# Inverse roots by one power on GpSimd in place of Newton steps on VectorE, in a fused cross-attention and FFN kernel

## The reference

```python
def _layernorm(x, axis=-1, eps=1e-05):
    m, v = mean(x), var(x)
    return (x - m) / sqrt(v + eps)

def simple_rmsnorm(x):
    n = maximum(norm(x, axis=-1), 1e-12)
    return x / n * sqrt(d)

def bitlinear158(x, w):          # rows to 8 bits by their largest value, weights to -1, 0, 1
    xn = simple_rmsnorm(x)
    return activation_quant(xn) @ weight_quant(w).T

x = x + cross_attention(layernorm(x), ctx)        # 16 heads, softmax over 64 keys
x = x + bitlinear158(gelu(bitlinear158(layernorm(x), w1)), w2)
```

## Time and profile before

| | us |
|---|---|
| median of 3 executions | 471.61 |
| the three executions | 467.57, 472.11, 471.61 |
| span of the profiled execution | 470.1 |
| PE busy in it | 399.1 (85%) |
| DVE busy | 344.6 (73%) |
| ACT busy | 257.7 (55%) |
| POOL busy | 218.9 (47%) |

### The profile page before, as it was taken

The page is one execution under the profiler, slowest core; times in us unless marked ns, Lnnn a source line. Parts: engine busy times, 40 slices in busy tenths (PEclk is TensorE's granted clock), DMA queues, the critical chain, the costliest instruction groups (busy, mean ns, idle before and its releaser), DMA issues.

```text
span 470.1 us, 8743 instructions
## 1 busy us (share of the span) xinstructions
PE 399.1 (85%) x2775; PEld 277.9 (59%) x2775; DVE 344.6 (73%) x909; ACT 257.7 (55%) x472; POOL 218.9 (47%) x269
## 2 busy tenths in 40 slices
PE   0998887989789897999999999999999997776463
PEld 0465754667557573767676767676767674464221
DVE  1805654788978896978787878787878788977663
ACT  0223244534276854676858585858485858555430
POOL 1000001445455474465655646474747474857551
PEclk9999998999899998999999999999999999999765
DMA  8950436431212323243425252434345343444435
GB/s 272 350 159 20 205 120 199 135 92 48 57 47 59 82 69 82 62 106 74 108 65 114 59 115 64 107 82 93 81 92 83 91 97 77 104 125 79 100 67 91
DMA packets 65085, 48.55 MB, mean 103 GB/s; under 512 B 51216, under 2 KB 56592, under 8 KB 64016
## 3 DMA queue, kind: packets, MB, share of 16 engines
q1 hardware_dynamic: 62656, 41.70, 36.4%
q10 hardware_dynamic: 2384, 6.29, 4.0%
HBM read 31.72 MB, written 4.46 MB: 77 GB/s over the span
## 4 chain that ended last, share of the span: by engine, by line
issue 41%; POOL 36%; PE 5%; DMA 3%; DVE 2%; POOLq 1%; SPq 1%; ACT 0%; DVEq 0%
POOL cl L529 10%; POOL tq L550 7%; POOL qb L553 6%; POOL yc L537 3%; POOL xa L542 3%; POOL xn L293 3%; POOL xq L545 3%; DMA qt<-qb 1%; DMA rinv_d<-ri 1%; DMA rb<-rinv_d 1%; POOLq L184 1%; PE hps L778 1%; PE ps L692 1%; PE ps L694 1%; PE hps L708 1%
## 5 line engine op out<-in xcount | busy, mean ns | idle before, releaser
L529 POOL TENSOR_TENSOR cl<-cr,ch 128x512 fp32r<-128x512 f32 x64 | 83.4, 1325 | 166.3 <-ACT ch L602 166.3
L692 PE MATMUL ps<-xh,ah 128*128 128x256 f32 x256 | 75.6, 295 | 7.1 <-ACT g L617 4.5
L746 PE MATMUL hps<-bh,ch 128*128 128x256 f32 x256 | 75.8, 296 | 1.3 <-POOL cl L529 1.3
L586 ACT ACTIVATE qf<-ps 128x512 f32<-128x512 f32 x64 | 37.5, 586 | 68.0 <-PE ps L694 68.0
L694 PE MATMUL ps<-xh,al 128*128 128x256 f32 x256 | 72.4, 283 | 0.0
L693 PE MATMUL ps<-xl,ah 128*128 128x256 f32 x256 | 72.3, 282 | 0.0
L748 PE MATMUL hps<-bh,cl 128*128 128x256 f32 x256 | 71.5, 279 | 0.0
L747 PE MATMUL hps<-bl,ch 128*128 128x256 f32 x256 | 71.4, 279 | 0.0
L602 ACT ACTIVATE ch<-cr 128x512 fp32r<-128x512 f32 x64 | 39.3, 631 | 56.8 <-DVE cr L866 56.8
L692 PEld LDWEIGHTS ps<-xh,ah 128*128 128x128 f32 x256 | 49.2, 192 | 29.2 <-issue 28.7
L778 PE MATMUL hps<-w2q,qt 128*128 128x256 bf16 x256 | 37.4, 295 | 19.8 <-DMA qt<-qb 15.1
(11 more groups left out here) (129 smaller groups left out, 812.3 us busy)
## 6 DMA issues: line engine op xcount, KB each, us to landing
rb<-rinv_d SPq DMA_DIRECT2D x64, 256.0 KB, 4.0
out<-yo SPq DMA_DIRECT2D x32, 128.0 KB, 3.8
wq_s<-wq ACTq DMA_DIRECT2D x2, 1024.0 KB, 12.1
wo_s<-wo_t SPq DMA_DIRECT2D x1, 2048.0 KB, 9.0
w_s<-w_t SPq DMA_DIRECT2D x2, 1024.0 KB, 5.3
xs<-x SPq DMA_DIRECT2D x2, 1024.0 KB, 5.0
xs<-x ACTq DMA_DIRECT2D x1, 1536.0 KB, 14.6
wk_a<-wk_t ACTq DMA_DIRECT2D x2, 512.0 KB, 9.2
```

The source lines that it names most:

```text
L529: pool.tensor_tensor(cl[:, u % 2, :, b * S:(b + 1) * S], cr[:, :, b * S:(b + 1) * S], ch[:, u % 2, :, b * S:(b + 1) * S].bitcast(F32), ALU ...
L692: pe.matmul(o, ah[:, c, cols], xh[:, k % 2, c, :], start=(c == 0), stop=False)
L746: pe.matmul(O[:, 0:D], c_h, bh[:, hp, :], start=(hp == 0), stop=False)
```

## The change

Both functions move from VectorE to POOL, and the shift and Newton steps become one `tensor_tensor` with the power operation, whose second operand is a tile of -0.5 (`mhalf`). The floor that was a tile (`least`) becomes a constant per half, so that the floor and the last multiplication are one instruction for each half. `norms` is now ahead of `x_round` in the same even steps; `reciprocal_deviations(1)` follows `norm_x` of tiles 2 and 3, and `(2)` is in step 12, between `norms(3)` and `x_round`. A step's norms are 4 or 6 instructions, x's deviations 4.

```diff
-        def reciprocal_deviations(dve, part):
+        def reciprocal_deviations(pool, part):
...
-            dve.tensor_scalar(nw[0][:, c], mv[:, c, 1], EPS_LN, None, ALU.add).then_inc(sem["rstd_steps"], 1)
-            dve.wait_ge(sem["rstd_steps"], n)
-            rsqrt(dve, nw[0][:, c], rstd[:, c], nw[1][:, c], sem["rstd_steps"], n)
-            dve.scalar_tensor_tensor(out=nmean[:, c], in0=mv[:, c, 0], scalar=-1.0, in1=rstd[:, c], op0=ALU.mult, op1=ALU.mult).then_inc(sem["rstd_steps"], 1)
+            pool.tensor_scalar(nw[0][:, c], mv[:, c, 1], EPS_LN, 1.0, ALU.add, ALU.mult).then_inc(sem["rstd_steps"], 1)
+            pool.tensor_scalar(nw[1][:, c], mv[:, c, 0], -1.0, 0.0, ALU.mult, ALU.add).then_inc(sem["rstd_steps"], 1)
+            pool.wait_ge(sem["rstd_steps"], n + 1)
+            pool.tensor_tensor(rstd[:, c], nw[0][:, c], mhalf[:, 0:c.stop - c.start], ALU.pow).then_inc(sem["rstd_steps"], 1)
+            pool.wait_ge(sem["rstd_steps"], n + 3)
+            pool.tensor_tensor(nmean[:, c], nw[1][:, c], rstd[:, c], ALU.mult).then_inc(sem["rstd_steps"], 1)
...
+                def norms(j):
...
+                    for h, floor in halves:
+                        pool.tensor_scalar(v[:, 2 * h:2 * h + 2], stat[:, j, 2 * h:2 * h + 2], floor, 1.0, ALU.max, ALU.mult).then_inc(done, 1)
+                    n += len(halves)
+                    pool.wait_ge(done, n)
+                    pool.tensor_tensor(r[:, c], v[:, c], mhalf[:, c], ALU.pow).then_inc(done, 1)
+                    pool.wait_ge(done, n + 1)
+                    pool.tensor_tensor(t[:, c], r[:, c], amax[:, j, c], ALU.mult).then_inc(done, 1)
+                    pool.wait_ge(done, n + 2)
+                    for h, floor in halves:
+                        pool.tensor_scalar(scl[:, j, 2 * h:2 * h + 2], t[:, 2 * h:2 * h + 2], EPS_Q, wfactor[:, h:h + 1], ALU.max, ALU.mult).then_inc(done, 1)
...
+                reciprocal_deviations(pool, 1)
                 for n in range(LAST):
+                    if n % 2 == 0 and 0 <= (n - 6) // 2 < NB + 2:
+                        norms((n - 6) // 2)
+                    if n == 12:
+                        reciprocal_deviations(pool, 2)
                     if n % 2 == 0 and tile(n - 6):
                         x_round(n - 6)
                         x_round(n - 5)
...
-                    if n % 2 == 0 and 0 <= (n - 6) // 2 < NB + 2:
-                        norms((n - 6) // 2)
-                    if n == 11:
-                        reciprocal_deviations(dve, 2)
                     if tile(n):
                         row_max(n)
```

More of the change, by code:

```diff
@@ L48 @@
 QC = 16
[L49 to L51 removed]
+RSTD_STEPS = 4
 KR = 8
@@ L55, with norm_count @@
 LAST = NT + 10
-NORM_STEPS = RSQRT_OPS + 3
+def norm_count(j):
+    return sum(6 if 2 <= i < NB else 4 for i in range(j + 1))
 def build(nc, x, kv, wq, wk_t, wqr, wkr_t, wkv, wo_t, w1_t, w2_t, consts, out):
@@ L91, in build @@
         stat, amax, scl = [sb(n, [P, NB + 2, 4], F32) for n in ("stat", "amax", "scl")]
-        least, wfactor = [sb(n, [P, 4], F32) for n in ("least", "wfactor")]
+        wfactor = sb("wfactor", [P, 2], F32)
+        mhalf = sb("mhalf", [P, 16], F32)
         level = sb("level", [P, 4], F32)
@@ L184, in at_least @@
                 e.wait_ge(s, value)
[L186 to L199, removed]
         XPARTS = [0, 4, 16, NT]
@@ L327, in _ @@
                 pool.memset(ones[:, :], 1.0).then_inc(sem["const_set"], 1)
-                for k, w in ((0, D), (1, F)):
-                    pool.memset(least[:, 2 * k:2 * k + 2], EPS_N ** 2 * (EPS_LN * D ** 2 if k == 0 else 1.0) / w).then_inc(sem["eps_set"], 1)
+                pool.memset(mhalf[:, :], -0.5).then_inc(sem["eps_set"], 1)
                 pool.memset(level[:, 0:2], -1.0 / 127.0).then_inc(sem["eps_set"], 1)
@@ L553, in g_round @@
                     pool.tensor_scalar(qb[:, t % 2, :], tq[:, :], 1.0, -MAGIC, ALU.mult, ALU.add).then_inc(sem["g_rounded"], 1)
+                def norms(j):
+                    c = slice(2 if j >= NB else 0, 2 if j < 2 else 4)
+                    halves = [(h, thr) for h, thr in ((0, LEAST1), (1, LEAST2)) if c.start <= 2 * h < c.stop]
+                    v, r, t = fw[0], fw[1], fw[2]
+                    done, n = sem["norm_steps"], norm_count(j) - 2 * len(halves) - 2
+                    if j == 0:
+                        pool.wait_ge(sem["w_mean_steps"], 2)
+                    if j < NB:
+                        pool.wait_ge(sem["x_squared"], 2 * j + 2)
+                        pool.wait_ge(sem["x_maxima"], 2 * j + 2)
+                    if j >= 2:
+                        pool.wait_ge(sem["g_squared"], 2 * j - 2)
+                        pool.wait_ge(sem["g_maxima"], 2 * j - 2)
+                    at_least(pool, done, n)
+                    for h, floor in halves:
[8 more added lines that the diff above has]
+                        pool.tensor_scalar(scl[:, j, 2 * h:2 * h + 2], t[:, 2 * h:2 * h + 2], EPS_Q, wfactor[:, h:h + 1], ALU.max, ALU.mult).then_inc(done, 1)
                 def ternary(k):
@@ L895, in g_scale @@
                     dve.reciprocal(c2[:, c], gm[:, c]).then_inc(sem["g_scale_steps"], 1)
[L897 to L901, removed]
[L902 to L914 removed]
                 def finish(t):
                     dve.wait_ge(sem["products"], t + 1)
[L918 removed]
+                    dve.wait_ge(sem["norm_steps"], norm_count(t // 2 + 2))
                     at_least(dve, sem[f"out_stored{t % 2}"], 16 * (t // 2))
@@ L927, in w_means @@
                     dve.tensor_scalar(wmean[:, 0:2], total, 1.0 / (F * D), EPS_Q, ALU.mult, ALU.max).then_inc(sem["w_mean_steps"], 1)
[L928 to L930 removed]
+                    dve.tensor_scalar(wfactor[:, 0:2], total, 1.0 / (F * D * 127.0), EPS_Q / 127.0, ALU.mult, ALU.max).then_inc(sem["w_mean_steps"], 1)
                     dve.wait_ge(sem["w_mean_steps"], 1)
                     dve.reciprocal(wscale[:, :], wmean[:, 0:2]).then_inc(sem["w_mean_steps"], 1)
[L933 removed]
+                    dve.wait_ge(sem["w_mean_steps"], 3)
                 def ternary(n):
```

38 lines of the change are left out of this document (11 added, 27 removed).

## The result

| | kernel before | changed kernel |
|---|---|---|
| median of 7 runs | 471.6 us (467.57 to 472.11) | 474.08 us (472.85 to 475.21) |
| profiled execution | span 470.1, clock 0.958 | 474.39, span 472.3, clock 0.958 |

The ratio is 1.0064 (95% interval 1.0037 to 1.009): the changed kernel is slower, by 3.0 us according to the ratio (2.5 between the medians), where 5.2 us less were forecast. VectorE's busy time fell from 344.6 to 293.9 us, as predicted; GpSimd's (POOL) rose from 218.9 to 263.3.

A forecast was written before the change was run, and what follows sets the result against it. PE was taken to bound the steady steps, with VectorE's inverse root just hidden there. The terms 0.6 - 0.7 - 0.4 + 4.3 - 0.8 + 0.7 + 1.5 gave 5.2 us gained, 471.6 to 466.4 us; range 462 to 480.

The forecast's parts named there:

- Part 1: Before the loop: part 0 of x's deviations is hidden by the weight stage on either engine, worth nothing.
- Part 2: Step 0: without the twelve-column inverse root VectorE takes the scores earlier, a gain of 0.6 us.
- Part 3: Step 11: 2.8 us of waiting at L768 and 1.5 us of low clock behind it vanish, together 4.3.
- Part 4: POOL, even steps: 2.0 us norms delay row maxima through SP's queue; steps 6, 8, 12 lose 0.7, 0.4, 0.8; 30 gains 0.7.
- The rooms: SP's queue: slack before POOL's delay reaches the row maxima; 0.9 us in step 6, 1.2 in 8, 3.7 in 14 to 28.
- rival A: POOL, head of even steps: slow power, passed on by SP's queue, makes it slower; 482 us at 4 us norms; chance 0.2.
- Part 5: Last steps: VectorE's maxima of g no longer wait behind an inverse root, a gain of 1.5 us.
- signs of being wrong: Power on POOL above about 1.5 us, new PE gaps before L728 in even steps, or step 11's wait persisting with another releaser.
- B: Step 12: the wait and clock loss of step 11 move here, so no change, 469.9 us; chance 0.25.

The follow-up runs named there:

- e4: Changed kernel with every power in norms and deviations replaced by a multiplication, so it computes other numbers: 464.37 us, ratio 0.9844.
- e2: Changed kernel with only the third part of the deviations (step 12) moved behind x_round, norms still ahead: 468.78 us, ratio 0.9969.
- e5: Changed kernel with SP's queue issuing the row maxima ahead of x's transposes in even steps 0 to 12, POOL untouched: 465.42 us, ratio 0.9897.
- e11: Changed kernel with the norms' power run once more into a spare tile in steps 14 to 28: 479.95 us, ratio 1.0194.
- e6: Changed kernel with norms and deviations behind x_round, and row maxima ahead of x's transposes in even steps 0 to 12: 461.11 us, ratio 0.9776.
- e8: Kernel before, with only SP's queue order changed: row maxima ahead of x's transposes in even steps 0 to 12: 472.67 us, ratio 1.0028.
- e12: Kernel before, with norms and deviations kept as Newton steps on VectorE but moved behind the residual: 547.53 us, ratio 1.1615.
- e7: Kernel before, with only the deviations moved to POOL (step 12 behind x_round), norms staying Newton steps on VectorE: 467.84 us, ratio 0.9917.
- e1: Changed kernel with norms and the third part of the deviations moved behind the two x_round calls of an even step: 461.15 us, ratio 0.9804.

## Why the prediction was wrong

The measured 474.1 us lies inside the stated range of 462 to 480, on the other side of the kernel before than the forecast: the range was wide enough, the sum had the wrong sign.

**Parts 1 to 3** hold. Part 1: the first power (four columns) took 1.02 us like the others and nothing shifted with it. The Trainium skill (GPSIMD Engine Reference, section 2.1, Instruction dispatch) has some 6 us for the first call to a freshly loaded kernel; no row shows it. Part 2: from the start of the scores of step 0 to the shift it takes 6.41 to 6.42 us in the four kernels with the twelve-column steps on VectorE and 5.84 to 5.89 us in the ten with them on POOL, 0.56 gained where 0.6 was predicted; only the whole time up to there varies too much to show it. Part 3: 2.8 us at L768 and 1.55 us of clock behind it measured, 2.8 and 1.5 predicted, with the same granted clock of 1.00 up to the next wait.

**Part 4 is the step that failed.** Its mechanism was the right one, a queue that hands POOL's delay to the row maxima, and its terms were too small, by three causes.
- The price of the power. Norms took 2.7 us (2.0 taken; 1.8 with one half, 1.6 taken), 16 columns with all that belongs to them 3.7 (2.5). I bounded the power by "a whole two-input operation of 512 columns" and took less, "as four columns are few"; a power is paid per column at some 70 times the price of that subtraction (158 against (1325 - 190) / 512 = 2.2 ns). e4 shows that this alone decides the sign.
- The rooms. Step 12 was priced at 0.8 and lost 2.9, none of which is left without the deviations ahead of x_round (e2). Here the room was right: with the measured prices the prediction's own sum gives 2.7 + 3.7 - 3.7 = 2.7. Step 8 was priced at 0.4 and lost 1.65: the transposes' issue took 3.44 us there instead of 2.51.
- The clock. Part 3 counted the clock behind a stall as won, and no term of part 4 counted it as lost behind a new one. From the shifts of steps 6, 12 and 30 to the next one the granted clock was 0.80, 0.86 and 0.84 (before: 0.86, 1.00 and 1.00), for 0.7, 1.7 and 1.1 us more. e2 shows the link for step 12. It is no fixed price: the kernel before waits 3.22 us in step 30 and keeps a clock of 1.00, and so does e5 after its 2.46 us.

Step 30 was given a gain of 0.7 and waits 0.16 us more than before. Steps 14 to 28 lost 0.4 us together, where nothing was predicted; e11 shows that the room is smaller in some steps: norms of 3.7 us, at which rival A still lost nothing, lost 6.0 us over the eight. The price beyond 3.7 us wasn't measured.

**Missing altogether:** the other small transfer behind the same transposes. In step 32 they hold back the reciprocal row sums, worth 3.7 us in the changed kernel's profile and 1.6 to 2.5 in three others. The prediction followed SP's queue to the row maxima and stopped there; the earlier trace rows stop two steps short.

**Part 5** was counted at 1.5; from the division of tile 31 to the end 2.3 us were regained. Relative to the last gelu POOL's first rounding starts 2.0 us earlier, as forecast, the second only 0.3, as the last norms stand between them.

All terms in the profile, from step 0 on: -0.9 in steps 1 to 5, +1.0 and +0.7 in step 6, +1.6 in step 8, -2.9 to step 11 (2.7 at the up-projection), -1.5 and +2.9 in step 12, +1.6 in step 13, +0.4 to step 29, +0.2 and +1.1 in steps 30 and 31, +3.6 up to the division of tile 31, -2.3 from there to the end. That is 5.5 us slower by these rounded terms, 5.4 by the table; this execution's shift of step 0 at 57.15 instead of 60.31 hides 3.2 of them, of which 0.6 are the gain of part 2 and the rest is the varying start. The 3.0 us of the timed runs lie between the 2.2 us of the two spans and these 5.4.

Two of the prediction's own signs of being wrong came: a power on POOL took more than 1.5 us (2.91 for 16 columns; 1.02 for four), and PE has new gaps ahead of the shift in steps 8, 12 and 26.

**The rivals.** B described what happened: "at step 11 the maxima leave in time, but step 12 now carries all of POOL's added work ... and PE waits there and loses its clock there instead". It was priced as no change, with 0.25, and had the right place and too short a list. A's threshold ("at about 3 us gain and loss cancel") was nearly right too; the 2.7 us of the norms lie just under it, and the division of tile 31 and the clock did the rest.

## What to carry to other kernels

When work moves to another engine, list everything that stands behind that engine in an in-order queue, to the last step of the kernel, and not only the transfer one has in mind; then look whether the moved work can stand behind what the queue waits for. Here the same instructions, three lines further down, turn +0.6% into -2%. Moving one small transfer ahead in the queue instead leaves the next one, the row sums, behind the transposes, and part of the wait goes over to it (e5, e6, e8). Price an operation that no row shows per column and not only per instruction, and count the clock behind each new wait as a possible loss, as it is counted behind each old one.

## What the runs showed of the hardware

- A power on GpSimd in fp32 with 128 partitions: 709, 1021, 2277 and 2914 ns for 2, 4, 12 and 16 columns; a multiplication: 194 to 221 ns.
- VectorE's small instructions beside a GpSimd instruction last until that ends: 1.2 us for one of 0.16 beside the subtraction of 512 columns (e12). The maxima of g (L888), a reduction, take 2.34 us beside it as without it. A free slot on VectorE isn't free where GpSimd is busy.
- The issue of two transposes on SP's queue takes 2.5 us at best and up to 4.1 (e7); a room worked out from one step isn't the room of all.
- A wait of PE of 2.9 us cost 1.7 us of clock behind it (granted 0.86 over 12.5 us, 1.00 without the wait in e2). Such waits don't always cost it: 3.22 us (step 30 before) and 2.46 us (step 13 of e5) were followed by 1.00. The clock also fell to 0.87 in a step of e6 whose longest wait, 1.03 us, is in e1 as well and was followed by 1.00 there, so not each drop is a wait's.
